# First layer of a two-layer attention and expert kernel: gate logits folded into two earlier matmuls, and the routing of a batch moved one step forward

## What is computed

```
q, k, v = split(x @ Wqkv)                       # 16 heads of 8 channels
q, k = rms_norm(q), rms_norm(k)
x1 = layernorm(x + softmax(q k^T / sqrt(8)) v @ Wproj + bproj)
logits = x1 @ gate_w.T                          # 16 experts
expert = argmax(logits); p = softmax(logits)    # top 1, at most CAP = 320 tokens an expert,
rank = cumsum(one_hot(expert)) - 1              # in the order of the tokens
out = p * (gelu(x1 @ w1[expert]) @ w2[expert])  # if rank < CAP
```

## Time and profile before

| | us |
|---|---|
| median of 3 runs | 884.03 (880.08 to 884.72) |
| the profiled execution, its own time | 883.63 |
| its span, first to last instruction | 881.9 |
| TensorE busy in the span | 775.9 (88%) |
| VectorE busy | 527.1 (60%) |
| ScalarE busy | 467.3 (53%) |
| GpSimd busy | 306.0 (35%) |

### The profile page before, as it was taken

One profiled execution on the slowest core, in us unless ns is written; L12 is line 12 of the kernel. 1 busy time (PEld: TensorE's weight loads), 2 busy tenths in 40 slices (PEclk: granted clock), 3 DMA queues, 4 the chain that ended last, 5 costly groups with the idle time before them and its releaser, 6 DMA issues.

```text
span 881.9 us, 19604 instructions
## 1 busy us (share of the span) xinstructions
PE 775.9 (88%) x7317; PEld 439.1 (50%) x7317; DVE 527.1 (60%) x1390; ACT 467.3 (53%) x743; POOL 306.0 (35%) x444
## 2 busy tenths in 40 slices
PE   1689999999928999479999999999999999999993
PEld 0234444444316777424555555555555555565441
DVE  4448888888441122255776647776665876545666
ACT  1487898889811222125544435554444555455575
POOL 3122443343337000234444325443334433224405
PEclk9999999999958999769999999999999999999997
DMA  1276333333205544131443244543335444222003
GB/s 28 75 236 157 105 98 103 106 101 97 64 31 130 153 141 140 54 89 49 103 100 71 52 88 103 103 102 72 70 73 96 103 91 92 56 55 54 2 1 96
DMA packets 111706, 78.05 MB, mean 89 GB/s; under 512 B 12272, under 2 KB 103088, under 8 KB 111616
## 3 DMA queue, kind: packets, MB, share of 16 engines
q1 hardware_dynamic: 106256, 70.38, 33.1%
q0 software_dynamic: 3344, 5.56, 2.5%
q10 hardware_dynamic: 2016, 0.92, 0.4%
HBM read 37.86 MB, written 13.63 MB: 58 GB/s over the span
## 4 chain that ended last, share of the span: by engine, by line
PE 34%; SPq 9%; DVE 6%; DMA 3%; issue 2%; ACT 1%; POOL 1%; ACTq 0%; DVEq 0%; POOLq 0%
PE l_ps_v L1287 7%; PE l_ps_c L1260 7%; SPq L115 4%; SPq L113 4%; PE l_ps_v L1188 4%; PE l_ps_d L1273 3%; PE l_by_query L1209 2%; DMA q_ring<-l_max_rows 2%; DVE l_rden L1839 2%; PE l_by_query L1200 2%; PE l_by_key L1242 1%; DVE l_neg_max L1827 1%; PE l_by_key L1380 1%; PE l_ps_m L1177 1%; PE l_ps_m L1380 1%
## 5 line engine op out<-in xcount | busy, mean ns | idle before, releaser
L1827 DVE TENSOR_REDUCE l_neg_max<-l_by_query 128x6 bf16<-128x768 f32 x125 | 119.7, 957 | 126.3 <-PE l_by_query L1213 125.6
L2107 POOL TENSOR_SCALAR_AFFINE_SELECT l_probs<-l_probs 128x512 f32<-128x512 f32 x128 | 88.2, 689 | 202.7 <-ACT l_probs L1533 202.4
L1533 ACT ACTIVATE l_probs<-l_by_key 128x768 f32<-128x768 f32 x128 | 103.8, 811 | 69.6 <-PE l_by_key L1245 65.4
L490 ACT ACTIVATE l_probs<-l_ps_s,minus_bound 128x1024 f32<-128x1024 f32 x128 | 137.2, 1118 | 2.4 <-PE l_ps_s L364 2.3
L1260 PE MATMUL l_ps_c<-l_probs,l_values 128*64 128x256 f32 (+1 forms) x1024 | 112.0, 340 | 0.0
L1260 PEld LDWEIGHTS l_ps_c<-l_probs,l_values 128*64 128x64 f32 x1024 | 62.3, 136 | 38.8 <-issue 19.6
L379 PE MATMUL l_ps_o<-l_probs,l_vpad 128*32 128x256 f32 x1024 | 78.9, 390 | 0.2 <-ACT l_probs L490 0.2
L1188 PE MATMUL l_ps_v<-w_v,l_xT 128*128 128x512 f32 x128 | 73.6, 657 | 0.4 <-ACT l_values L1554 0.4
L1554 ACT ACTIVATE l_values<-l_ps_v 128x512 f32<-128x512 f32 x64 | 38.2, 597 | 66.9 <-PE l_ps_v L1188 64.5
L1287 PE MATMUL l_ps_v<-w_o,l_ctx 128*128 128x128 f32 x512 | 66.9, 285 | 0.0
L2115 POOL DMA_INDIRECT l_eg<-eout_d,fetch x32 | 34.4, 1076 | 90.3 <-POOLq L836 82.7
(11 more groups left out here) (263 smaller groups left out, 1438.0 us busy)
## 6 DMA issues: line engine op xcount, KB each, us to landing
l_rrep<-rden_d SPq DMA_DIRECT2D x32, 512.0 KB
q_ring<-l_parts SPq DMA_DIRECT2D x192, 64.0 KB
k_ring<-l_parts SPq DMA_DIRECT2D x180, 64.0 KB
w_both<-in_L_ffn_w_dram SPq DMA_DIRECT2D x32, 256.0 KB, 3.1
disp_d<-zeros SPq DMA_DIRECT2D x8, 320.0 KB, 3.5
l_xin<-in_L_attn_x_dram SPq DMA_DIRECT2D x16, 128.0 KB, 2.5
l_xr<-in_L_attn_x_dram SPq DMA_DIRECT2D x16, 128.0 KB, 2.4
x_d<-l_x SPq DMA_DIRECT2D x16, 128.0 KB, 2.1
```

What stands on the lines that cost most here:

```text
L490: act.activation(probs[c % RING][:, :], ps_s[c % 2][:, :], ACT.Exp, bias=k["minus_bound"][:, :], scale=SCALE).then_inc(probs_sb, 1)
L1533: act.activation(probs[c % P_RING][:, :, 0:N + P], by_key[:, :, 0:N + P], ACT.Exp, scale=SCALE).then_inc(p_sb, 1)
L1827: dve.tensor_reduce(neg_max[:, :, half, :, h].rearrange("p a u -> p u a"), query_scores(b, c)[:, :, 0:3 * P].rearrange("p u (a q) -> p u a ...
L2107: pool.affine_select(out=corners, in_=corners, compare_op=ALU.is_ge, fill=0.0, base=0, pattern=[[0, 4], [1, P]], channel_multiplier=-1).th ...
```

## The change

The logits are made in another way. The gate's weights have their mean over channels taken out (in `constants`), so that the logits of y - mean(y) equal those of y. As y = x + att @ Wproj + bproj, its logits are x @ gate + att @ (Wproj @ gate) + bproj @ gate. The first term comes from 16 more columns of `w_val` (the values' matmul, 144 columns instead of 128), the second from 16 more columns of `w_proj`, the third is a row of constants, `gate_bias`. The logits are no longer multiplied by rstd; the argmax does not need it, and the exponentials are now taken once at the end, after a multiplication with the rstd of all batches.

ScalarE copies x's share out of PSUM (`of_x`, four buffers), GpSimd adds `gate_bias`, VectorE adds the projection's share (`logits`). The transposes of x1, their copy and the logit matmuls go. All routing of a batch is now done in the step after its attention (b-1), one step earlier than before, and there is one step less at the end. In VectorE's list the normalised keys are finished first (`normalised`), then come y, logits, gates, then the split, and only then the statistics.

The core of the diff:

```diff
@@ constants: mean over channels out of the gate's weights
+            pe.wait_ge(step, 5)
+            pe.matmul(gps[:, E:2 * E], k["ones"][:, :], k["gate_T"][:, :], start=True, stop=True).then_inc(gate_turned, 1)
...
+            dve.wait_ge(gate_turned, 2)
+            s.did(dve.scalar_tensor_tensor(k["gate_T"][:, :], gps[:, E:2 * E], -1.0 / C, k["gate_T"][:, :], ALU.mult, ALU.add))
@@ l0_layer, TensorE: columns of w_proj once, then no transposes of x1 and no logits
+                        if b == -2:
+                            pe.wait_ge(w_in, W_IN)
+                            pe.transpose(ps_b[:, 0:P], w_proj[:, 0:C], ident[:, :]).then_inc(fold_ps, 1)
+                            pe.wait_ge(fold_sb, 2)
+                            pe.matmul(ps_b[:, 0:E], attT[:, 0:P], k["gate_T"][:, :], start=True, stop=True)
+                            pe.matmul(ps_b[:, E:2 * E], attT[:, P:2 * P], k["gate_T"][:, :], start=True, stop=True)\
+                              .then_inc(fold_ps, 1)
...
-                            last = pe.matmul(ps_b[:, j * C:(j + 1) * C], attT[:, j * P:(j + 1) * P], w_proj[:, :],
+                            last = pe.matmul(ps_b[:, j * VG:(j + 1) * VG], attT[:, j * P:(j + 1) * P], w_proj[:, :],
...
-                    if c == GATES_AT and real(b - 2):
-                        for j in range(NB):
-                            last = pe.transpose(ps_b[:, j * P:(j + 1) * P], x1[p][:, j, :], ident[:, :])
-                        last.then_inc(x1T_ps, 1)
-                    if c == GATES_AT + 1 and real(b - 2):
-                        pe.wait_ge(x1T_sb, b - 1)
-                        for j in range(NB):
-                            last = pe.matmul(ps_b[:, j * E:(j + 1) * E], x1T[:, j * P:(j + 1) * P], k["gate_T"][:, :],
-                                             start=True, stop=True)
-                        last.then_inc(logit_ps, 1)
...
-                    if c == CHUNKS - 1 and real(b - 2):
-                        pe.wait_ge(gate_step, (b - 1) * GATE)
+                    if c == CHUNKS - 1 and real(b - 1):
+                        pe.wait_ge(gate_step, b * GATE)
@@ ScalarE
+            act.dma_start(b_col[:, :], bproj.unsqueeze(1)).then_inc(w_in, 16)
...
-                    if c == GATES_AT and real(b - 2):
-                        act.activation(x1T[:, :], ps_b[:, 0:N], ACT.Copy).then_inc(x1T_sb, 1)
...
-                    if c == CHUNKS - 1 and real(b - 2):
-                        act.activation(ex[:, (b - 2) * NB:(b - 1) * NB, :], below[:, :, :], ACT.Exp).then_inc(exp_sb, 1)
...
+                        act.activation(of_x[(b + 1) % 4][:, :, :],
+                                       ps_a[1][:, 0:NB * VG].rearrange("p (j c) -> p j c", c=VG)[:, :, C:VG],
+                                       ACT.Copy).then_inc(of_x_in, 1)
...
+            act.wait_ge(weight_step, 1)
+            act.activation(below, below, ACT.Exp).then_inc(exp_sb, 1)
@@ VectorE, in step
+                if real(b + 2):
+                    normalised(b + 2, p)
                 if real(b - 1):
...
+                    all_logits(b - 1)
+                if real(b - 1):
+                    gates(b - 1)
...
-                if real(b - 2) and real(b):
-                    ranks(b - 2)
-                    routes(b - 2, hb - 1, p)
+                if real(b - 1) and real(b):
+                    ranks(b - 1)
+                    routes(b - 1, (b - 1) // 2, o)
...
-            unrolled(step, 2, 2)
+            unrolled(step, 2, 1)
@@ GpSimd, after the low part
+                if real(b + 1):
+                    pool.wait_ge(of_x_in, b + 2)
+                    pool.tensor_tensor(of_x[(b + 1) % 4][:, :, :], of_x[(b + 1) % 4][:, :, :],
+                                       gate_bias[:, :].unsqueeze(1).broadcast_to([P, NB, E]), ALU.add).then_inc(of_x_set, 1)
-                if real(b - 2):
-                    at_least(pool, rank_step, (b - 1) * RANK)
+                if real(b - 1):
+                    pool.wait_ge(ln_step, b * LN)
+                    pool.wait_ge(rank_step, b * RANK)
```

More of the change, by code:

```diff
@@ L586, in over_rms, with normalised @@
                 s.did(dve.reciprocal(nr_t[:, :], rms[:, :]))
+            def normalised(b, p):
+                over_rms(b)
+                s = norm
+                s.wait()
+                at_least(dve, qkT_ps, b - 1)
+                for j in range(NB):
+                    scale = nr_t[:, 2 * H * j:2 * H * (j + 1)].rearrange("p (s h) -> p s h", h=H // 2)
+                    s.did(dve.tensor_tensor(qkn[p][:, j, :].rearrange("p (s w h) -> p s h w", s=4, h=H // 2),
+                                            ps_a[j][:, 0:2 * C].rearrange("p (s h w) -> p s h w", s=4, w=HD),
+                                            scale.unsqueeze(3).broadcast_to([P, 4, H // 2, HD]), ALU.mult))
+                s.wait()
+                for j in range(NB):
+                    kn = qkn[p][:, j, C:2 * C].rearrange("p (r w h) -> p r w h", r=2, h=H // 2)
+                    s.did(dve.tensor_tensor(kn, kn, k["qks"][:, :].unsqueeze(1).unsqueeze(3).broadcast_to([P, 2, HD, H // 2]),
+                                            ALU.mult))
+                s.end()
@@ L588, in gates, with all_logits @@
+            def all_logits(b):
+                s = gate.batch(b)
+                dve.wait_ge(of_x_set, b + 1)
+                s.did(dve.tensor_tensor(logits[:, :, :], ps_b[:, 0:NB * VG].rearrange("p (j c) -> p j c", c=VG)[:, :, C:VG],
+                                        of_x[b % 4][:, :, :], ALU.add))
             def gates(b):
[L590 to L593 removed]
+                s = gate
@@ L594, in gates @@
                 s.wait()
-                at_least(dve, exp_sb, b)
-                s.did(dve.tensor_tensor(below[:, :, :], lg, over(top[:, :], E), ALU.subtract))
+                s.did(dve.tensor_reduce(top[:, :], logits[:, :, :], AX.X, ALU.max))
                 s.wait()
-                s.did(dve.scalar_tensor_tensor(cand[:, :, :], below[:, :, :], 0.0, each(k["backwards"][:, :]),
-                                               ALU.is_ge, ALU.mult))
+                here = below[:, b * NB:(b + 1) * NB, :]
@@ L600, in gates @@
+                s.did(dve.tensor_tensor(here, logits[:, :, :], over(top[:, :], E), ALU.subtract))
+                s.wait()
+                s.did(dve.scalar_tensor_tensor(cand[:, :, :], here, 0.0, each(k["backwards"][:, :]), ALU.is_ge, ALU.mult))
                 s.wait()
@@ L635, in weights @@
             def weights():
-                s = Steps(dve, weight_step, 3).batch(0)
-                dve.wait_ge(exp_sb, B)
-                s.did(dve.tensor_reduce(esum[:, :], ex, AX.X, ALU.add))
+                s = Steps(dve, weight_step, 4).batch(0)
+                dve.wait_ge(pow_step, B * POW)
+                s.did(dve.tensor_tensor(below, below, over(rstd[:, :], E), ALU.mult))
+                dve.wait_ge(exp_sb, 1)
+                s.did(dve.tensor_reduce(esum[:, :], below, AX.X, ALU.add))
                 s.wait()
```

133 lines of the change are left out of this document (61 added, 72 removed).

## The result

The changed kernel took 877.33 us (median of six runs, 874.72 to 881.09), the kernel before 884.83 us beside it (six runs, 880.08 to 885.46). The ratio is 0.992, with a 95% interval of 0.989 to 0.994: 7.5 us less, where 9.9 were forecast. The predicted 873.7 us is 3.6 too low, and the range of 868.5 to 880.5 holds the result.

What follows compares the result with a forecast made beforehand. TensorE was taken to bound the middle of the layer, with VectorE close behind. From 883.63 us, +1.5 (start) - 5.6 (middle) - 1.5 (steps 14 and 15) - 4.3 (end) gave 873.7 us, range 868.5 to 880.5.

Steps and rivals of the forecast that it cites:

- The start: Up to the first layer's fill: a longer `constants` and one more transfer ahead of ScalarE's table load cost +1.5 us.
- The middle: Eleven middle steps of the layer: each falls from 12.91 to 12.4 us, a gain of 5.6 us.
- TensorE's own work: Middle step, first of three bounds: 0.87 us less work on TensorE, leaving 12.0 us a step.
- VectorE's list: Middle step, second bound: VectorE's operations back to back, with GpSimd's holds, take 12.0 to 12.3 us.
- The loop through both engines: Middle step, third bound: from `rden` through the normalised keys and their transposes to the next `rden`, 12.15 us.
- The 0.25 us on top of it: Middle step: with three loops so close, lateness is rarely made up, so 12.4 us was taken.
- Steps 14 and 15: Last two steps, without keys to normalise: TensorE's 0.87 us counts nearly in full, a gain of 1.5 us for both.
- The end: End of the layer: only batch 15's routing is left, the last `sidx` ends earlier, a gain of 4.3 us.
- TensorE keeping the whole gain (1): Middle steps: VectorE slips through between GpSimd operations, step 12.0 to 12.1, 869.8 us in all; chance 0.15.
- The lock eating the middle (2): Middle steps: GpSimd's root and residual addition hold VectorE, step 12.9, 879.2 us and up to 881; chance 0.2.
- Scatters holding VectorE (3): Middle steps: scatters beside the next step's roots make the kernel slower, 891.3 us at a step of 14.0; chance 0.05.
- The end's new tail (4): End of layer: VectorE and ScalarE's new last operations end the block instead of the scatters, 875 to 878 us; chance 0.1.

Runs made afterwards that it cites:

- few scatters: Kernel before with the scatters of batches 0 to 12 left out (26 of 32): 875.98 us, ratio to before 0.997.
- repeat: The changed kernel run once more, unaltered, on another chip: 869.13 us, ratio to before 0.991.
- repeat profile: The kernel before run again, unaltered, for a second profile, on the chip of the changed kernel's third profile: 879.19 us, ratio 0.999.
- y first: Changed kernel with y ahead of the normalisation again, logits and gates still behind the keys: 874.28 us, ratio to before 0.993.
- third profile: The changed kernel again, unaltered, beside the kernel before on the same chip: 872.28 us, ratio to before 0.991.
- low part first: Changed kernel with GpSimd computing the keys' low part ahead of `veps` and the root: 868.51 us, ratio to before 0.987.
- first pair of profiles: The profiled executions of the kernel before (883.63 us) and of the changed kernel (881.09 us, the slowest of its six).

## Why the prediction came out as it did

**The measured gain agrees with undelayed traces.** Before and changed kernel on the same chip, term by term: table load ahead of the first `xT` copy +1.37; to the third `rden` -1.16; eleven middle steps 137.57 to 133.82, **-3.75**; two more 20.76 to 19.20, **-1.56**; last `rden` to the experts 21.91 to 18.52, **-3.39**; the rest +3.21. The second and the last differ by some us between executions of one kernel: over the three profiles of before (few scatters among them) and the three of the changed kernel (first, repeat and third), the way from the first `rden` to the third is 28.4 to 30.4 and 26.9 to 29.9 us, the part from the experts on 614.0 to 615.4 and 613.1 to 617.6. Without them the sum is -7.3, and the measured ratios (0.992, 0.991, 0.991) make it 7.3 to 8.3 us.

**The start** (+1.5 forecast, 1.37 and 1.35 measured). The transfer cost 0.5 us where 0.73 was taken, which leaves 0.87 for the constants, estimated at 0.8.

**The middle is the step that failed**: eleven steps, from 12.91 to 12.4. Four things in it, all of size:

- *The base was wrong.* It took TensorE's own step as 142.00 divided by 11, 12.91. From `rden` to `rden` the profile had 140.54 over eleven, 12.78; and of this, the undelayed kernel needs 12.51 on average, 12.57 in a plain step. The earlier trace rows had said so: busy 137.65 of 142, with 4.35 us of idle time that the text passed over by calling TensorE the bound. In 2.3 us of it TensorE waited for what ScalarE had yet to make, above all the exponentials behind a late copy, and in the repeat profile these waits are gone (0.4 us are left); no row of the prediction showed them. Two of the three bounds inherited it, TensorE's own work and VectorE's list, both reckoned down from 12.91.
- *The loop through both engines was right.* Forecast 12.15, measured 12.12; its wait on `qkn` is there, at 0.34 us a step, and y first lengthens wait and step together. That it fits to 0.03 us is partly luck: the transposes start 6.00 us after `rden` where 5.9 was forecast, and from there to the next `rden` it takes 6.12 us where 6.24 was. The latter is 6.16 in both profiles of before; the delays lie ahead of the transposes, so the wrong base cancels here. VectorE's list, put at 12.0 to 12.3, takes 12.12 with nearly no idle time in it.
- *TensorE's own work was put too high.* Forecast 12.0 of 12.91; by its busy share it fell from 12.45 us a step to 11.72 (107.98 and 105.42 of 109 us), which is 0.73 us less where 0.87 was forecast. This bound didn't set the step, so the size didn't matter.
- *The 0.25 us on top of it was not needed.* "An engine that is late in one step is rarely early in the next" gave 12.4. The plain steps repeat to 0.03 us, and with the odd ones (12.16 to 12.46 us in the third profile) the average is 12.17. That adds 0.05 us, and not 0.25, to the plain 12.12. The lock on `sidx`, which was to bring VectorE to 12.0 to 12.3, costs the plain step nothing (low part first).

So, between undelayed profiles, the middle's term was worth 3.75 us and not 5.6, and in the profile shown first it is hidden by delays of over 1.1 us in seven hand-overs.

**Steps 14 and 15**: 1.5 forecast, 1.56 measured. The 3.10 of the first pair of profiles is this and, for the most part, two delays of before (0.92 and 0.46 us) that the changed kernel doesn't have there.

**The end**: from y to the last `sidx` it fell from 9.56 to 5.26 us, **4.30** as forecast. Two things eat 0.9 of it, so that 3.39 is left. y comes 0.22 later after `rden`, where 0.13 was allowed. This is mostly the moment at which the granted clock falls, and not the width: the last projection takes 0.71 us in the repeat of before, at 1.00, and 0.93 in the third profile, where the clock falls to 0.50 within it, behind 4 us in which TensorE was busy 1.88; in the first pair it is 1.02 us before and 0.76 after the change, the other way round. And from the last `sidx` to the experts it takes 10.51 instead of 9.81 us: GpSimd issues the last scatters 0.79 us after `sidx` ends instead of 0.28, and the first of them takes 1.06 instead of 0.96. "The scatter, the barrier and the experts' first load behind it stay as they were" is the sentence that failed; why GpSimd picks up that wait later wasn't tried. Between the two profiles of before the whole piece differs by 1.05 us (22.96 and 21.91), so the 3.39 is known to about 1 us.

**The rivals.** TensorE keeping the whole gain (1) didn't happen, for the reason given by the loop and not by the lock. The lock eating the middle (2) is refuted for the root and for the plain step: low part first takes the lock off `sidx` and the step stays. Its other half, the residual's addition landing beside the gates or the cast, did happen, in one to five of the eleven steps of an undelayed profile, at 0.1 to 0.6 us each. The small operations beside `rstd` keep their 0.15 to 0.18 us, as `choices` did in the earlier trace rows, against the Trainium skill's rule ("SBUF — State Buffer", section on who interferes with whom), by which every GpSimd operation that reads SBUF should exclude them; L785, L778 and the residual's addition (L774) agree with it. Scatters holding VectorE (3): the roots beside them run at 0.22 to 0.23 us as ever, and leaving the scatters out changes no plain step. The end's new tail (4) finished at 255.1 us, with the experts' first matmul at 262.95.

**What stays open**: where the delays of the first two profiles come from. They lie near GpSimd's scatters, they hit both kernels, and on four other occasions, on three chips, ten profiles of kernels with all their scatters have none. One can say that the order of the instructions alone doesn't set them. Whether that chip, that hour or something in its memory did it, these runs can't tell. The kernels' medians went with it: 884.8 and 877.3 us there, 878 to 881 and 869 to 872 elsewhere, which is some 6 us for both and leaves their ratio alone. Nor do the runs say how often the 1.5 us delays of the changed kernel occur on that chip; its other five runs, 874.7 to 878.2, were all faster than the profiled one.

## What to carry to other kernels

Before a bound is reckoned from an engine that is "97% busy", ask who owns the other 3%: a wait that a hand-over took 0.3 us too long in is not work, and no edit to the work will shorten it. Take the period of a steady loop from one instruction to its own repeat, and prefer a repeat profile of the unchanged kernel to a finer reading of one. When two engines hand work to each other once a step, count the loop through both; the place of one 0.42 us operation in the other engine's list took back 0.28 of the 0.45 us a step that the change had brought. A lock that stretches an operation on an engine with slack can be left alone, but it uses the slack up: here the list with the lock just filled the step, and every further hold went into the step's length.

## What the runs showed of the hardware

- A hand-over from TensorE to an idle ScalarE took 0.04 us in every step of some executions and 0.15 to 1.80 us in others of the same kernel, near GpSimd's indirect transfers; the cause stays open. In the delayed ones TensorE lost up to 1.3 us at the next instruction that needed the copy.
- GpSimd's 128x512 operation held a small VectorE operation with two SBUF inputs (128x2 or 128x32) until its own end, for up to 1.18 us, wherever it was put (`sidx`, `choices`, L660, L663); beside `rden`, `att` and the reduction of the squares it held nothing. The root, 0.72 us on 128x2, held none of the operations that ran beside it.
- The residual's addition on GpSimd (128x256, 0.73 us) held `l_hot_bf` (0.75 instead of 0.19 us) and the cast of 128x512 (0.93 instead of 0.43 us) in the steps in which it met them.
- 26 scatters left out of 32 shortened no plain step, but the way from the last `sidx` to the experts by 2.2 and 2.3 us.
